# Expert layers: an empty slot gathers the token of its partition's number instead of token 0

## The reference

```python
# layer 0: K = 6 experts a token, E = 64, CAP = 128 slots an expert
scores = softmax(xf @ gate_w.T)
_, idx = top_k(scores + gate_b, K)
...
xb = zeros((E, CAP, D)).at[se, pos].set(xf[tok], mode='drop')
h = silu(einsum('ecd,eid->eci', xb, w1)) * einsum('ecd,eid->eci', xb, w3)
yb = einsum('eci,edi->ecd', h, w2)
...
y = zeros_like(xf).at[tok].add(contrib * wf[:, None])

# layer 1: TOPK = 8 experts a token, E = 64
x_sorted = x_flat[tok]                       # tokens sorted by expert
g = ragged_dot(x_sorted, we_gate, group_sizes)
u = ragged_dot(x_sorted, we_up, group_sizes)
o = ragged_dot(silu(g) * u, we_down, group_sizes)
y = zeros_like(x_flat).at[tok].add(o * w_sorted[:, None])
```

## Time and profile before

| | |
|---|---|
| median of 3 runs | 2411.56 us (2410.48 to 2414.87) |
| the profiled execution | 2412.86 us |
| its span, first to last instruction | 2411.2 us |
| mean granted TensorE clock | 0.889 |
| busy: PE, DVE, POOL, ACT | 1873.5, 1563.1, 1241.5, 1024.7 us |
| layer 0, first input gather to last | 959.3 to 1142.3 us |
| layer 1, first input gather to last | 1844.3 to 2205.4 us |
| layer 1, first output gather | 2226.93 us |

### The profile page before, as it was taken

One profiled execution on the slowest core, in us unless ns is written; L12 is line 12 of the kernel. 1 busy time (PEld: TensorE's weight loads), 2 busy tenths in 40 slices (PEclk: granted clock), 3 DMA queues, 4 the chain that ended last, 5 costly groups with the idle time before them and its releaser, 6 DMA issues. The chain is left out here.

```text
span 2411.2 us, 38801 instructions
## 1 busy us (share of the span) xinstructions
PE 1873.5 (78%) x11288; PEld 1301.1 (54%) x11289; DVE 1563.1 (65%) x3375; ACT 1024.7 (42%) x2930; POOL 1241.5 (51%) x1000
## 2 busy tenths in 40 slices
PE   5699978888888668999579999699548999988000
PEld 5378843343433243677437878588414888876000
DVE  5599928999999968333537777477686333333633
ACT  1467637666656323333037777343215333332000
POOL 1488616766666610788305555366002554543775
PEclk9799988999999977999879999899665999999555
DMA  7311013212111052998511110100503999998332
GB/s 211 96 73 73 8 44 130 102 40 93 48 72 69 0 166 60 230 294 199 141 34 32 32 37 24 29 1 2 188 0 98 286 282 281 275 252 202 110 116 84
DMA packets 163804, 272.04 MB, mean 113 GB/s; under 512 B 28722, under 2 KB 97300, under 8 KB 162708
## 3 DMA queue, kind: packets, MB, share of 16 engines
q1 hardware_dynamic: 130708, 199.72, 25.4%
q0 software_dynamic: 30464, 68.19, 12.4%
q10 hardware_dynamic: 2496, 2.44, 0.4%
HBM read 218.74 MB, written 51.53 MB: 112 GB/s over the span
## 5 line engine op out<-in xcount | busy, mean ns | idle before, releaser
L1017 POOL TENSOR_TENSOR b_h<-b_h,b_bcb 128x1024 f32<-128x1024 f32 x128 | 301.9, 2358 | 151.4 <-DVE b_h L1074 150.8
L1573 POOL DMA_INDIRECT m1x_xb<-scratch_xn,m_tok x192 | 183.0, 953 | 330.9 <-DVE m1x_yb L1702 173.7
L842 PE MATMUL b_psy<-b_h,ident 128*128 128x512 f32 x512 | 252.8, 621 | 69.5 <-POOL b_h L1017 69.2
L1074 DVE TENSOR_TENSOR_SCAN b_h<-b_dA,b_pbx 128x1024 f32<-128x1024 f32 x128 | 292.6, 2286 | 4.4
L1620 PE MATMUL m1x_psh<-m1x_xe,m1x_w 128*128 128x128 f32 x1536 | 211.8, 282 | 23.8 <-DMA m1x_w<-in_m_w 20.9
L1689 DVE TENSOR_TENSOR m1x_hT<-m1x_sg,m1x_psh 128x128 f32<-128x128 f32 x192 | 55.2, 287 | 240.3 <-ACT m1x_sg L1672 143.9
L1620 PEld LDWEIGHTS m1x_psh<-m1x_xe,m1x_w 128*128 128x128 f32 x1536 | 190.7, 195 | 34.5 <-issue 22.2
L842 PEld LDWEIGHTS b_psy<-b_h,ident 128*128 128x128 f32 x512 | 93.6, 194 | 210.3 <-POOL b_h L1017 123.3
L973 ACT ACTIVATE b_dA<-b_delta,b_A 128x504 f32<-128x504 f32 x256 | 166.8, 706 | 93.3 <-DVE b_h L1074 87.8
L1883 POOL TENSOR_TENSOR x_s<-x_s,x_rs 128x1024 f32<-128x1024 f32 x64 | 121.1, 1893 | 127.5 <-DVE x_rs L2049 127.4
L1068 DVE TENSOR_TENSOR b_pbx<-b_pdx,b_bcb 128x1024 f32<-128x1024 f32 x128 | 157.6, 1231 | 20.9 <-ACT b_pdx L956 14.8
(11 more groups left out here) (449 smaller groups left out, 4401.6 us busy)
## 6 DMA issues: line engine op xcount, KB each, us to landing
m1x_w<-in_m_w SPq DMA_DIRECT2D x192, 256.0 KB
b_bcb<-scratch_bc_rows SPq DMA_DIRECT2D x64, 512.0 KB, 4.8
scratch_y<-m1x_yb SPq DMA_DIRECT2D x192, 128.0 KB
m_w<-in_m_w SPq DMA_DIRECT2D x64, 368.0 KB
a_c<-in_ctxT SPq DMA_DIRECT2D x16, 512.0 KB, 3.6
m_w<-in_m_w SPq DMA_DIRECT2D x64, 128.0 KB
x_c<-in_ctxT SPq DMA_DIRECT2D x32, 256.0 KB
m_w2all<-in_m_w SPq DMA_DIRECT2D x1, 8192.0 KB
```

The costliest lines, as they stand in the source:

```text
L842: mm = pe.matmul(psy[:, k % 2, :], ident[:, :], h[:, u % HB, j, :], start=False, stop=(nq == NQ - 1 and j == CQ - 1))
L1017: q.tensor_tensor(hs, hs, bcb[:, 1, CQ * nq:CQ * nq + CQ], ALU.mult).then_inc(sem("hc"), 1)
L1074: v.tensor_tensor_scan(h[:, u % HB].rearrange("p j n -> p (j n)"), dA[:, u % DB].rearrange("p j n -> p (j n)"), pbx[:, :, :].rearrange("p ...
L1573: g.indirect_dma_start(out=xb[:, j, :], out_offset=None, in_=xn, in_offset=bass.IndirectOffsetOnAxis(ap=tok[:, b:b + 1], axis=0)).then_inc ...
```

## The change

An empty slot used to name token 0 for its gather, by a maximum with 0. Now it names the token whose number is that of its partition. Like `dest`, `tok` is made in two steps: a column of slots that holds the partition's number plus one where the table has 0, and then that column less one plus the table. The rows of taken slots and all of `dest` are as before. What an empty slot computes goes to the same places as before, which no token reads.

```diff
-            nodest = r.sb("nodest", [P, 1])
+            nodest, notoken = r.sb("nodest", [P, 1]), r.sb("notoken", [P, 1])
...
                     v.tensor_scalar(nodest[:, :], iotab[:, 0:1], float(T + 1), None, ALU.add)
+                    v.tensor_scalar(notoken[:, :], iotab[:, 0:1], 1.0, None, ALU.add)
                     step(v.tensor_copy(tokf[:, :], tokid[:, :]))
...
                     v.wait_ge(rs("at_used"), NT * K)
 
-                    step(v.tensor_scalar(tok[:, :], table, -1.0, 0.0, ALU.add, ALU.max))
+                    v.tensor_scalar(slotv[:, 1, :], table, 0.0, notoken[:, 0:1], ALU.is_equal, ALU.mult).then_inc(rs("empty"), 1)
                     step(v.tensor_scalar(slotv[:, 0, :], table, 0.0, nodest[:, 0:1], ALU.is_equal, ALU.mult))
+                    v.wait_ge(rs("empty"), 1)
+                    step(v.scalar_tensor_tensor(tok[:, :], slotv[:, 1, :], -1.0, table, ALU.add, ALU.add))
                     step(v.scalar_tensor_tensor(dest[:, :], slotv[:, 0, :], -1.0, table, ALU.add, ALU.add))
```

## The result

The changed kernel takes 2398.46 us (median of 6 runs, 2396.43 to 2404.99) against 2413.22 us for the kernel before (6 runs, 2409.73 to 2418.82). The ratio is 0.9943, with a 95% interval of 0.9928 to 0.9958. The span of the profiled execution is 2394.8 us, 16.4 less than before.

What follows compares the result with a forecast made beforehand. It took the DMA engines, held by gathers of one row, to bound layer 1's empty blocks. Terms -14.0 - 1.0 + 0.8 = -14.2 us took the median 2411.56 to 2397 us; main case 2390 to 2404, with the shared case 2389 to 2408.

Steps and rivals of the forecast that it cites:

- not the gather: Rival, layer 1's empty blocks: rereading the same expert's weights holds up the memory; 2412.4 us, chance 0.09.
- both: Rival, layer 1's empty blocks: gathers and weights share the blame, half of 14.0 us comes; 2405.4 us, chance 0.08.
- slower: Rival, layer 0's nearly empty experts: 128 different rows cost more engine time than one open row; 2427 us, chance 0.05.
- Saved in the blocks after 2140 us: Layer 1's last 35 blocks: faster gathers in the 33 empty blocks save 14.0 us; bounds nothing and 19.1 us.
- the middle stretch's pace: Layer 1: 1.887 us a block before the change, taken as the pace the last 35 blocks would reach, from 2.286.
- Partly empty blocks: Layer 1's blocks with 25 empty slots on average: 1 us saved, between nothing and PE's 7.1 us of weight waits.
- the two terms: Layer 1 savings: 14.0 us from the blocks after 2140 us and 1.0 us from the partly empty blocks.
- The added work: End of both routers: one more DVE operation each, 0.45 us in layer 1 and 0.32 in layer 0, 0.8 us together.
- the two columns: Early in each router: the new column `notoken` costs 146 ns a layer; counted only in the upper end, 1.1 us.
- The rule of the Trainium skill: Rule against the forecast: equal bytes cost equal time whatever addresses are read, so no gain, 2412.4 us.
- The cover: Layer 0's expert blocks: PE at 2.76 and POOL at 3.18 us a block hide faster transfers, so nothing gained.

Runs made afterwards that it cites:

- e1: Changed kernel, but layer 1's empty slots gather token 0 again; layer 0 stays changed: 2400.52 us, ratio 1.0008 to the kernel before.
- e3: Changed kernel, but in layer 1 only the wholly empty blocks' slots name different tokens, the other empty slots token 0: 2381.38 us, ratio 0.9917 to the kernel before.
- e4: Kernel before (token 0), but layer 1's 33 empty blocks load weights of experts 0 to 32 in turn: 2400.37 us, ratio 1.0010 to the kernel before.
- e2: Changed kernel, but layer 0's empty slots gather token 0 again; layer 1 stays changed: 2387.14 us, ratio 0.9934 to the kernel before.
- e5: Changed kernel, but empty slots of both layers name tokens 0 and 1 alternately (two rows, 64 readers each): 2397.34 us, one run.
- e10: Changed kernel, but each four neighbouring partitions' empty slots name the same token (32 rows), both layers: 2390.05 us, one run.
- e9: Changed kernel, but empty slots of partitions 0 to 63 name token 0, those of 64 to 127 token 1, both layers: 2396.80 us, one run.

## Why the prediction was right

**The cause.** Gathers of one row by all 128 partitions held the DMA engines, and through them the weights for which PE waited. The rates in the earlier trace rows pointed to it, and e1, e3 and e4 show it: undoing layer 1 alone brings back the whole loss, mending the 33 wholly empty blocks alone is enough for the gain, and changing the weights alone changes nothing. That the delay reaches PE through the weights is read from PE's waits (13.7 us before, 2.0 now); no run tests this step by itself. The rivals "not the gather" and "both" fall with e4, and "slower" with e2 and the 298 GB/s above.

**The terms.** Saved in the blocks after 2140 us: predicted 14.0 us at the middle stretch's pace. The real pace was 1.818, below that of the middle, so 35 x (2.286 - 1.818) = 16.4 us, and the times of the last 38 outputs say the same, 85.9 - 69.6 = 16.3 us. They also repeat well: 84.3 and 85.8 us in e1 and e4, 69.0, 69.0 and 68.8 in e2, e3 and e5. Why the empty blocks run a little faster than full ones was not tried. Partly empty blocks: predicted 1 us, which is below what the runs resolve. The 154th output comes 293.7, 289.0, 290.0 and 287.6 us after the first gather with token 0 in their empty slots (before, e1, e4, e3) and 291.8, 288.4 and 292.2 us without (changed kernel, e2, e5), and the middle stretch went from 1.887 to 1.869 us, but e4 has 1.869 with token 0 as well. PE's waits for weights from 1860 to 2140 us are a little longer with token 0 (7.1, 9.4, 7.8 and 6.7 us) than without (4.4, 4.5 and 4.4), and the pace does not follow them. The expert part as a whole gave 18.2 us where the two terms made 15.0; of the 18.2, 1.9 us come before the 154th output, within that scatter.

**The added work.** The timeline of DVE at the end of both routers:

```profile
958.83 0.28 DVE L1497 TENSOR_SCALAR m0r_slotv<-m0r_psc,m0r_notoken 128x64 f32<-128x64 f32 x1 [0.33 <-PE m0r_psc L1315]
959.03 0.28 DVE L1498 TENSOR_SCALAR m0r_slotv<-m0r_psc,m0r_nodest 128x64 f32<-128x64 f32 x1
959.34 0.22 DVE L1500 SCALAR_TENSOR_TENSOR m_tok<-m0r_slotv,m0r_psc 128x64 uint32<-128x64 f32 x1
...
1844.19 0.42 DVE L1497 TENSOR_SCALAR m1r_slotv<-m1r_psc,m1r_notoken 128x192 f32<-128x192 f32 x1 [0.27 <-PE m1r_psc L1315]
1844.52 0.41 DVE L1498 TENSOR_SCALAR m1r_slotv<-m1r_psc,m1r_nodest 128x192 f32<-128x192 f32 x1
1844.96 0.35 DVE L1500 SCALAR_TENSOR_TENSOR m_tok<-m1r_slotv,m1r_psc 128x192 uint32<-128x192 f32 x1
1845.35 0.35 DVE L1501 SCALAR_TENSOR_TENSOR m_dest<-m1r_slotv,m1r_psc 128x192 uint32<-128x192 f32 x1
```

The new operation takes 0.33 us of the chain in layer 1 (1844.19 to 1844.52) and 0.20 in layer 0 (958.83 to 959.03), less than the 0.45 and 0.32 of the earlier trace rows. The kernel has no wait directly behind it, and the next one starts before its recorded end (958.83 + 0.28 and 1844.19 + 0.42). So 0.5 us and not 0.8.

**The sum, and luck in it.** Layer 1's first gather starts 2.6 us later than before (1844.35 to 1846.90), and 1.7 of these stand already at layer 0's first gather (959.26 to 960.98). The 0.5 us and the two columns are the smaller part; the rest is a difference between executions, whose start of layer 1 lies anywhere from 1843.3 us (e10) to 1852.7 (e2). In the span, 18.2 us saved, less 2.6, and 0.7 us less after the first output gather, make 16.4; between the medians it is 14.8, with 14.2 predicted. The mechanism was right and the main term 2.4 us too small. That the total came within 0.6 us is in part luck, since a difference between executions, which the prediction has no term for, went the other way.

**The rule of the Trainium skill.** The Trainium skill's page "DMA: Bandwidth & Descriptors", section "Anatomy of one DMA — SWDGE (gpsimd) path", gives a transfer's time as a fixed part and its bytes over a fixed rate. The measurement decides otherwise: 119 and 314 GB/s of queue 0's own time for the same 128 KB a block, by the row numbers alone. In layer 0, where queue 0 is alone, a gather of 160 KB lands 5.8 us (median) after its issue in e4, with token 0, and 2.9 us in e3, with different rows; a part of the 5.8 may be a wait behind the gathers before it.

**The cover.** Layer 0 was costed at nothing, since PE and POOL take longer than the DMA. e1 and e2 confirm it, and in the changed kernel POOL still issues a gather every 3.18 us (1083.63 and 1086.81). The cover is large: queue 0 at 111 instead of 298 GB/s is not felt.

## What to carry to other kernels

Padding that all 128 readers take from one address was not free here: spread it over more rows (two were enough in e5 and e9) before looking at the bytes. Read each queue's rate by its own busy time; a queue whose MB per busy microsecond falls while its neighbour's nearly stays is the one to suspect, and the wait appears at whatever queues behind it. Then ask what sets the pace where the fault was never present: here that was one queue that issued both weights and stores, and moving the stores was worth more (22.7 us of the expert part) than the change itself (18.2).

## What the runs showed of the hardware

In the windows shown, gathers of one row ran at 109 to 127 GB/s of queue time whatever else was in flight: 115 with nothing beside it in layer 0, 119 beside the weights in layer 1, 109 in e4. With two rows or more the windows shown give 288 to 328 GB/s.

A limit of about 115 GB/s on what one row can give would explain both; it is a guess that no run tests. In layer 0's 5 us window POOL issues a gather of 160 KB every 1.25 us by the timeline (966.81 to 968.06 before the change), 131 GB/s, which is above one such limit and below two. What moved in these 5 us fits: 0.50 MB, 100 GB/s, before the change, and 0.66 MB, 132 GB/s, after it, all that POOL issues. But two rows gave 328 GB/s of the queue's own time in e5, above twice 115, so the guess holds only if the packets of a gather are spread over the 1.25 us. It would also explain why blocks with some real rows between them cost nothing. Which part of the memory sets it, and whether 100 or 120 readers of one row are already too many, was not tried.
